# A graph layer on one Trainium2 core: key marks stored tile by tile, keys turned by the tensor engine, and set-up work moved behind the first slot marks

## What is computed

```python
msg = jax.nn.relu(node_inputs[src] + edge_inputs)
agg = jax.ops.segment_sum(msg, dst, num_segments=N_NODES)
h = (1.0 + eps[0]) * node_inputs + agg
x = _layernorm(x + h @ W.T + b, axis=-1)
```

## Time and profile before

| | us |
|---|---|
| median of three runs | 2077.78 (2077.75 to 2079.56) |
| the profiled execution's own time | 2076.23 |
| its span, first to last instruction | 2074.0 |
| PE busy | 2012.9 (97%) |
| PE weight loads | 1920.2 (93%) |
| DVE busy | 1649.0 (80%) |
| ACT busy | 1566.4 (76%) |
| POOL busy | 1517.5 (73%) |

### The profile page before, as it was taken

How to read it: one execution, slowest core, us unless ns; L and a number is a source line. 1 busy time by engine, 2 the same in 40 slices (tenths; PEclk the granted TensorE clock), 3 DMA queues, 4 the chain that set the end, 5 groups by cost and what they waited for, 6 DMA issues and landing times. The chain is left out here.

```text
span 2074.0 us, 117127 instructions
## 1 busy us (share of the span) xinstructions
PE 2012.9 (97%) x46449; PEld 1920.2 (93%) x46449; DVE 1649.0 (80%) x4231; ACT 1566.4 (76%) x1616; POOL 1517.5 (73%) x1571
## 2 busy tenths in 40 slices
PE   2999999999999999999999999999999999999997
PEld 2899999999999999999999999999999999999994
DVE  6888888878888888877888888877888888887885
ACT  5777777777777777777777777777777777777774
POOL 6477777777777777777777777777777777777770
PEclk9999999999999999999999999999999999999998
DMA  6344444444544444444444444444444444444441
GB/s 157 86 112 109 110 111 110 113 114 115 112 111 110 110 111 110 114 112 112 116 111 110 110 110 111 114 113 112 115 112 110 109 110 111 111 115 112 115 112 35
DMA packets 236283, 228.68 MB, mean 110 GB/s; under 512 B 104218, under 2 KB 185556, under 8 KB 236062
## 3 DMA queue, kind: packets, MB, share of 16 engines
q1 hardware_dynamic: 183023, 200.99, 33.5%
q0 software_dynamic: 50080, 25.74, 12.7%
q10 hardware_dynamic: 3154, 1.60, 0.4%
HBM read 225.43 MB, written 2.71 MB: 110 GB/s over the span
## 5 line engine op out<-in xcount | busy, mean ns | idle before, releaser
L536 POOL DMA_INDIRECT rows_all<-in_x,index x1565 | 1517.0, 969 | 507.1 <-issue 474.0
L1173 PE MATMUL found<-table,oh 128*128 128x128 bf16 x18720 | 1241.0, 225 | 11.4 <-issue 3.1
L1173 PEld LDWEIGHTS found<-table,oh 128*128 128x128 bf16 x18720 | 1167.9, 144 | 43.6 <-issue 21.2
L1008 ACT ACTIVATE oh<-keys,minus_lanes 128x1024 bf16<-128x1024 f16 x195 | 224.2, 1150 | 310.3 <-PE found L1173 294.4
L1154 PE MATMUL l<-xparts,oh 128*57 128x96 bf16 x18720 | 436.5, 207 | 0.9 <-ACT oh L996 0.9
L1154 PEld LDWEIGHTS l<-xparts,oh 128*57 128x57 bf16 x18720 | 409.7, 108 | 14.1 <-issue 1.1
L989 ACT ACTIVATE oh<-slots,minus_lanes 128x1824 bf16<-128x1824 f16 x195 | 351.3, 1801 | 0.0
L781 DVE COPY_PREDICATED rows_all<-mask,found 128x256 f32<-128x256 uint16 x780 | 343.3, 440 | 7.6 <-issue 1.4
L964 ACT CAST table<-l 128x768 bf16<-128x768 f32 x390 | 311.1, 798 | 40.2 <-PE l L1154 26.0
L996 ACT ACTIVATE oh<-oh 128x1824 bf16<-128x1824 bf16 x195 | 335.7, 1721 | 0.0
L775 DVE TENSOR_TENSOR mask<-iota,side 128x32 f16<-128x32 f16 x195 | 37.6, 193 | 305.2 <-PE found L1173 290.1
(11 more groups left out here) (126 smaller groups left out, 904.4 us busy)
## 6 DMA issues: line engine op xcount, KB each, us to landing
slots<-slot_dram SPq DMA_DIRECT2D x195, 456.0 KB
msg<-in_edge SPq DMA_DIRECT2D x390, 128.0 KB
keys<-key_dram SPq DMA_DIRECT2D x195, 256.0 KB
rows_all<-in_x,index POOLq DMA_INDIRECT x1565
index<-in_src SPq DMA_DIRECT2D x195, 4.0 KB
key_dram<-key SPq DMA_DIRECT2D x195, 2.0 KB
slot_dram<-slot_row SPq DMA_DIRECT2D x195, 3.6 KB
oh<-in_x SPq DMA_DIRECT2D x3, 512.0 KB, 6.5
```

The costliest lines, as they stand in the source:

```text
L536: pool.indirect_dma_start(to, None, x, bass.IndirectOffsetOnAxis(indices[:, j:j + 1], 0)).then_inc(done, 16)
L1008: nc.scalar.activation(key_marks(b), by_edge(keys[:, four, :]), ACT.Square, bias=minus_lanes[:, b:b + 1]).then_inc(keys_squared, 1)
L1173: last = nc.tensor.matmul(found[:, t * FOUND:(t + 1) * FOUND], key_marks(b)[:, :, t], table[:, b, n * FOUND:(n + 1) * FOUND],  start=(b == ...
```

## The change

Four things are edited together.

- Key marks: `oh2` is now P x KEYS x COLS with no pitch; keys, and so marks, are in order of tile and then edge, so a tile's 128 marks are one run of 256 bytes. DVE and ACT read and write runs.
- Keys on PE: DVE writes the 8 keys into the first 8 of 32 columns of one `key` tile, which has one buffer where it had two. In `fill_slots` PE multiplies it with the identity, which turns it into `key_ps` (32 x 128) beside `slot_ps` in PSUM. ACT copies both at once (32 x 185 where it was 32 x 57). SP writes keys and slots to DRAM after that copy; `spread_keys` is gone. DVE no longer waits for the key write of two rows back; ACT does.
- Set-up order: DVE does `place_nodes` and `prepare_weights` at the end of step -1, behind the slot marks of row 0; the three `describe_chunk` calls move from the ends of steps -2, 0 and 1 to those of 0, 1 and 2. PE's `prepare_weights` moves from step -2 to step 0, behind `look_in_buckets`.
- Loads and clears: the load of x for the output (`x_sb`) moves from ACT's queue to SP's at the end of step -1; ACT's last two `clear_sums` move to the ends of steps 0 and 1.

```diff
-        oh2 = sb("oh2", [P, KEYS, P * PITCH], BF16)
+        oh2 = sb("oh2", [P, KEYS, COLS], BF16)
...
+        key_ps = ranks[0:BUCKETS, 256:256 + P]
+        slot_ps = ranks[0:BUCKETS, 256 + P:256 + P + CAP]
+        turned_ps = ranks[0:BUCKETS, 256:256 + P + CAP]
...
         def key_marks(b):
-            return oh2[:, b, :].rearrange("p (e t) -> p e t", t=PITCH)[:, :, 0:LOOK]
+            return oh2[:, b, :]
...
-            def spread_keys(st):
-                if has(st, 2, ROWS):
...
-                    sp.wait_ge(key_ready, r + 1)
-                    sp.dma_start(key_dram[four].rearrange("(p t) -> p t", t=LOOK), key[:, two, :]).then_inc(key_written, 16)
...
             def spread_slots(st):
...
                     sp.wait_ge(slots_copied, r + 1)
-                    sp.dma_start(slot_dram[four].rearrange("(b c) -> b c", c=CAP), slot_row[:, two, :]).then_inc(slots_written, 16)
+                    sp.dma_start(key_dram[four].rearrange("(t p) -> t p", p=P), turned_row[0:LOOK, two, 0:P]).then_inc(key_written, 16)
+                    sp.dma_start(slot_dram[four].rearrange("(b c) -> b c", c=CAP), turned_row[:, two, P:P + CAP]).then_inc(slots_written, 16)
...
             def step(st):
                 load_index(st)
-                spread_keys(st)
                 load_edges(st)
                 spread_slots(st)
+                if not st.inside and st.s == FROM + 2:
+                    sp.wait_ge(nodes_ready, 2 * SPANS)
+                    for p0, p1 in shares(NP):
+                        sp.dma_start(x_sb[p0:p1, :, :], x_v[p0:p1, :, :]).then_inc(x_loaded, 16)
...
                         split_x()
+                    if st.s == FROM + 2:
+                        place_nodes()
                         prepare_weights()
-                        place_nodes()
-                        describe_chunk(0)
-                    if st.s == FROM + 2:
                         take_all_nodes()
-                    if 0 <= st.s < 2:
-                        describe_chunk(st.s + 1)
+                    if 0 <= st.s < 3:
+                        describe_chunk(st.s)
...
                     act.wait_ge(slots_ready, r + 1)
-                    nc.scalar.copy(slot_row[:, two, :], slot_ps).then_inc(slots_copied, 1)
+                    nc.scalar.copy(turned_row[:, two, :], turned_ps).then_inc(slots_copied, 1)
...
-                    clear_sums(2)
-                    clear_sums(3)
+                if not st.inside and 0 <= st.s < 2:
+                    clear_sums(st.s + 2)
...
-                                found[:, t * FOUND:(t + 1) * FOUND], key_marks(b)[:, :, t],
+                                found[:, t * FOUND:(t + 1) * FOUND], key_marks(b)[:, t * P:(t + 1) * P],
...
                     wait_count(pe, slots_copied, r)
+                    nc.tensor.matmul(key_ps, key[:, :], ident_half[:, :], start=True, stop=True)
                     for t in range(LOOK):
```

More of the change, by code:

```diff
@@ L48, in gnn_kernel @@
     EARLY_KEYS = 2
-    PITCH = LOOK + 2
     WINDOW = 40
@@ L77, in gnn_kernel @@
     ZRING = 4
+    assert LOOK * BUCKETS <= 256 and P + CAP <= 192 and LOOK <= BUCKETS
     assert SHORT <= POOLED and WINDOW <= P and LOOK % 2 == 0
@@ L146, in gnn_kernel @@
         counts = sb("counts", [P, LOOK, BUCKETS], F16)
-        key = sb("key", [P, 2, LOOK], F16)
+        key = sb("key", [P, BUCKETS], F16)
         in_slot = sb("in_slot", [P, LOOK, CAP], F16)
         placed = sb("placed", [P, LOOK, BUCKETS], F16)
-        slot_row = sb("slot_row", [BUCKETS, 2, CAP], F16)
+        turned_row = sb("turned_row", [BUCKETS, 2, P + CAP], F16)
         mask = sb("mask", [P, 2, LOOK, SIDE], F16)
@@ L213, in gnn_kernel @@
         y_sb = xparts[0:NP, :, :, :].rearrange("p b n f -> p (b n f)").bitcast(F32)[:, 0:NT * P].rearrange("p (t c) -> p t c", c=P)
-        src_rows = oh2[:, :, :].rearrange("p b c -> p (b c)").bitcast(I32)[:, 0:2 * COLS].rearrange("p (h c) -> p h c", h=2)
+        src_rows = oh2[:, :, :].rearrange("p b c -> p (b c)").bitcast(I32).rearrange("p (h c) -> p h c", h=2)
         rel_rows = src_f[:, :, :].rearrange("p h c -> p (h c)").bitcast(F16).rearrange("p (h c) -> p h c", h=2)
@@ L228, in gnn_kernel @@
         rank_ps = ranks[:, 0:LOOK * BUCKETS].rearrange("p (t b) -> p t b", b=BUCKETS)
-        slot_ps = ranks[0:BUCKETS, 384:384 + CAP]
+        key_ps = ranks[0:BUCKETS, 256:256 + P]
+        slot_ps = ranks[0:BUCKETS, 256 + P:256 + P + CAP]
+        turned_ps = ranks[0:BUCKETS, 256:256 + P + CAP]
         rank_iota = ranks[:, 448:448 + CAP]
@@ L397, in key_marks @@
         def key_marks(b):
-            return oh2[:, b, :].rearrange("p (e t) -> p e t", t=PITCH)[:, :, 0:LOOK]
-        def by_edge(values):
-            return values.rearrange("p (e t) -> p e t", t=LOOK)
+            return oh2[:, b, :]
         def turned_sources(k):
@@ L476, in load_edges @@
                         sp.dma_start(msg[slot][:, POOLED * D:ROW], one(edge_spans[1], b - 1)).then_inc(edges_loaded[slot], 16)
-            def spread_keys(st):
-                if has(st, 2, ROWS):
-                    r, two, four = st.s + 2, slot_of(st, 2, 2), slot_of(st, 2, RING)
-                    sp.wait_ge(key_ready, r + 1)
-                    sp.dma_start(key_dram[four].rearrange("(p t) -> p t", t=LOOK), key[:, two, :]).then_inc(key_written, 16)
             def spread_slots(st):
@@ L582, in _ @@
             nc.vector.memset(ones[:, :].bitcast(U16), 0x3C00)
+            nc.vector.memset(key[:, :].bitcast(U16), 0)
             nc.vector.memset(one_row[:, :], 1.0)
@@ L737, in give_key @@
                     r = st.s + 2
-                    wait_count(dve, key_written, (r - 1) * 16)
                     dve.wait_ge(rank_ready, r + 1)
-                    nc.vector.tensor_tensor(key[:, slot_of(st, 2, 2), :], of_row(bucket, r), of_row(key_base, r), ALU.add).then_inc(key_ready, 1)
+                    nc.vector.tensor_tensor(key[:, 0:LOOK], of_row(bucket, r), of_row(key_base, r), ALU.add).then_inc(key_ready, 1)
             def give_slots(st):
@@ L765, in mark_keys @@
                     wait_count(dve, blocks_looked, (r - 1) * KEYS + (b + 1))
-                    nc.vector.tensor_scalar(key_marks(b), by_edge(keys[:, four, :]), lanes[:, b:b + 1], None, ALU.is_equal).then_inc(oh2_ready, 1)
+                    nc.vector.tensor_scalar(key_marks(b), keys[:, four, :], lanes[:, b:b + 1], None, ALU.is_equal).then_inc(oh2_ready, 1)
             def mark_sides(st):
@@ L969, in copy_slots @@
                     wait_count(act, slots_written, (r - 1) * 16)
+                    wait_count(act, key_written, (r - 1) * 16)
                     act.wait_ge(slots_ready, r + 1)
-                    nc.scalar.copy(slot_row[:, two, :], slot_ps).then_inc(slots_copied, 1)
+                    nc.scalar.copy(turned_row[:, two, :], turned_ps).then_inc(slots_copied, 1)
             def relu(st):
@@ L1007, in square_keys @@
                     wait_count(act, blocks_looked, (r - 1) * KEYS + (b + 1))
-                    nc.scalar.activation(key_marks(b), by_edge(keys[:, four, :]), ACT.Square, bias=minus_lanes[:, b:b + 1]).then_inc(keys_squared, 1)
+                    nc.scalar.activation(key_marks(b), keys[:, four, :], ACT.Square, bias=minus_lanes[:, b:b + 1]).then_inc(keys_squared, 1)
             def mark_keys(st):
@@ L1032, in step @@
                     round_x(1, x_mid)
-                    act.wait_ge(nodes_ready, 2 * SPANS)
-                    for p0, p1 in shares(NP):
-                        act.dma_start(x_sb[p0:p1, :, :], x_v[p0:p1, :, :]).then_inc(x_loaded, 16)
-                    clear_sums(2)
-                    clear_sums(3)
+                if not st.inside and 0 <= st.s < 2:
+                    clear_sums(st.s + 2)
             steps(act, step)
@@ L1239, in step @@
                 if not st.inside and st.s == 0:
+                    prepare_weights()
                     turn_nodes()
@@ L1253, in step @@
                 if not st.inside and st.s == FROM + 1:
-                    prepare_weights()
                     place_kept()
```

## The result

The changed kernel takes 2130.6 us in the median of four runs (2123.5 to 2135.2) against 2077.8, also of four: a ratio of 1.0248, 95% interval 1.0232 to 1.0264. It is slower; 2046.6 was forecast, with 2077 as the upper end. Its profiled execution has a span of 2121.2 us and a time of 2123.5.

The account below looks back on a forecast made before the run. PE was taken to bound the kernel, with POOL close behind and the bound after the change: 69.2 + 1908.3 + E (30) + 3.3 + 32.0 gave a span of 2042.8 us, 2046.6 as time, range 2027 to 2077.

Parts of the forecast that it names:

- 5.1 forecast: look_in_table on PE: quicker weight loads from runs gain 5.1 ns per matmul (bounds 0 and 7), 0.49 us per step.
- the prediction's reading of it: Weight loads of look_in_table: by the skill's rule stride costs nothing; as a rival, time 2081 us, chance 0.11.
- The start: Set-up before the loop: first look_in_table matmul 10.1 us earlier, 1.6 given back, so POOL's long run gains 8.5 us.
- the 32.4 in that sum: Set-up: the time in us from which PE can look in the buckets, where it was 44.65.
- E: POOL's long run of gathers: time added by hold-ups, 30 us, with 6 below and 81 above as bounds.
- The sum of the prediction: Whole span: 69.2 + 1908.3 + E + 3.3 + 32.0, or 2012.8 + E, giving 2042.8 us.
- 17 for the phase: Part of E once DVE waits for POOL in a fixed phase: 0.1 us in each of 165 steps.
- the 6 of the medians: Lower bound and first part of E: 6 us, as the median gather is 4 ns over the least.
- today's 39 / 192: Hold-ups of gathers in the kernel before, 0.2 us per step, taken as the upper end for the fixed phase.
- that 3.3: From the last gather's end to its use by DVE's addition of gathered rows: an estimated 3.3 us.
- collisions eat it: Rival: L733 or L797 holds up a gather by 0.3 us each step, E = 63, time 2080 us; chance 0.14.
- the loop of the slots: Rival: the slots' way over ACT and SP bounds the step at 10.5 us, time 2134 us; chance 0.10.

Follow-up runs that it names:

- first experiment: The kernel before with only the set-up order of the change (DVE, PE, ACT and SP ahead of the loop): 2072.9 us, ratio 0.9976.
- halves and 6 zeros: The changed kernel with DVE's slot and key marks each cut in two instructions and 6 matmuls of zeros per row on PE: 2098.9 us, ratio 1.0105.

## Why the prediction was wrong

**What held.** The weight loads of L1168 last 98 ns, as L1211's did (ns min/median/max, 400 to 1500 us):

```profile
L1168 PEld LDWEIGHTS found<-table,oh x10062: 95/98/99, 401.4 to 1500.0; 128*128 128x128 bf16 x198
L1168 PE MATMUL found<-table,oh x10061: 218/219/229, 401.4 to 1500.0; 128*128 128x128 bf16 x198
```

The starts of its matmuls are 56.0 ns apart in the mean, 61.2 before, and hardly vary (5% and 95% at 55 and 56, before 57 and 67). That is 5.2 ns for 5.1 forecast, and PE's step 9.714 for 9.73. The Trainium skill (TensorE: Matmul & The Clock Gate, Weight-path perf modes) lists "packed or strided" as the fast load's read pattern and names no difference in time between the two. That they cost the same was the prediction's reading of it, and it does not hold in this case: 142 against 98 ns. The start held as well:

```profile
33.52 0.73 PE L1149 MATMUL l<-xparts,oh 128*57 128x96 bf16 x13 [0.83 <-ACT oh L995]
...
46.67 1.54 PE L1168 MATMUL found<-table,oh 128*128 128x128 bf16 x13 [1.59 <-ACT table L962]
...
69.19 1.19 POOL L534 DMA_INDIRECT rows_all<-in_x,index  x1 [7.36 <-PE found L1168]
```

POOL's long run starts at 69.19 and not 77.74, 8.55 us earlier for 8.5. The way there was less exact: the first L1168 comes at 46.67 and not 45.2 (the 32.4 in that sum should be 28.6 + 3.5 = 32.1; measured is 33.5). That POOL then bounds the kernel and DVE waits for it at L796 also came.

**The term that failed is E**, the hold-ups of the gathers, "E = 6 + 7 + 17 = 30". The sum of the prediction with what was measured: 69.2 + 1908.3 + E + (2121.2 - 2084.7 = 36.5, for 35.3) = 2121.2 gives E = 107: 103 of hold-ups and 4 of a gap behind PE near 94 us, which no part of the sum had:

```profile
94.49 1.16 POOL L534 DMA_INDIRECT rows_all<-in_x,index  x1 [4.39 <-PE found L1168]
```

That is 77 us over the 30, and above the 81 that was called the upper bound. Of the 103, some 15 fall in the first 40 steps, and 88 in the rest, where the sum had 17 for the phase and most of the 6 of the medians. E failed in three ways.

- The list of instructions that hold a gather was too short. I counted L733 and L797, which read two SBUF tiles, and left out the marks by `tensor_scalar` (L753, L765), because in the trace before most gathers that ran beside them were not longer. They were not, because in the phase in which POOL rested against L733 nearly all began too soon after a mark's start: of 154 with 0.16 us or more of a slot mark ahead of them 151 began within 0.016 us of its start, and of 212 at a key mark 189 began 0.067 to 0.079 us after its start. None of these was held. 62 of the 103 us come from marks. The Trainium skill, GPSIMD Engine Reference, Specifications, names both kinds: two SBUF inputs, and instructions in a 2-port perf mode. I took half of that sentence. The trace does not name an instruction's mode; if the marks run in such a one, the 93 hold-ups by L753 and 90 by L765 agree with the rest of it.
- The phase was taken as "today's 39 / 192" at the worst. That 0.2 us is the delay of a POOL that is pushed back to PE's pace and would go faster if let; it is no measure of what DVE does to a POOL that lags. A gather that starts somewhere in an instruction of length L waits L/2, and it does so in L / 1.245 of the cases. Summed over the slot marks (2 x 0.64), the key marks (3 x 0.52), L796 (0.72) and L732 (0.42), the squares over 2 x 1.245 are 0.93 us per step; measured is 103 / 192 = 0.54. POOL's step would be 10.9 by the first and is near 10.5 by the second, not 10.1. So this estimate is 1.7 times too high here: the starts don't fall evenly, and those just behind a mark's start are not held.
- The place of L797 was misjudged, in the rival's own "against". It had DVE wait until 3.3 us behind the last gather, between two starts; that 3.3 was borrowed from the landing of the slot load. In the changed kernel the addition begins 1.51 us behind the end of the batch's last gather (median of 134 steps from row 60 on). The second gather after that one begins after 0.305 + 0.94 + 0.305 = 1.55 us, so the addition falls right on a gather's start: in the step above at 1012.77 against 1012.79. When it comes some 0.05 us or more ahead, it holds the gather: 73 times, 0.44 us each in the mean.

The rival "collisions eat it" was the right mechanism with too small a price. Its 0.3 us per step were 0.54, and the time from there 2012.8 + 103 + 4 + 3.5 = 2123, that of the profiled run (the 3.5 are 1.2 of a longer end and 2.3 from the span to the time). The rival whose time fits best, the loop of the slots with 2134, is wrong: with seven gathers the same loop runs at 9.714. ACT waits for slots once in the changed kernel (7.1 us, at the start) and three times with seven gathers (9.2 us in all, 7.3 of it in one wait). A number that fits is no proof of its cause.

Small errors: "never slower that I can see" was said of the key marks; L765 takes 541 ns in the mean for 495 before, since POOL and DVE hold each other up. The start's gain reached POOL in full, but with the loop unchanged only 4 of 8.5 us are left at the end (first experiment).

## What to carry to other kernels

An engine whose gaps are all "issue" and all alike (0.305 us between gathers here) has no slack in them: add the gap to each instruction before you call the next engine the bound, and ask at what pace the present bound hides it. Where two engines share a path, a lagging one can cost more than a slower first one; here six matmuls of zeros, 0.33 us more of PE per step, make the changed kernel 3.4% faster (0.9903 / 1.0248). Before a bound is handed to an engine that shares a path, sum over the instructions that can hold it, each with its length squared over twice the pace (1.7 times too high here, but nearer than a phase guessed from before), and take none out because it did no harm in the old phase.

## What was not expected of the hardware

- Each hold-up ends with one DVE instruction: the gather's end lies 0.815 us (within 0.025 in 268 of 268) behind that instruction's end. In other runs most do, not all: 197 of 198 in the kernel before, some 350 of 400 with halves and 6 zeros. It must have begun a little before the gather, and how much differs: L796 holds from 0.047 us on and not up to 0.044, the key mark L765 from 0.073 on and not up to 0.076. The addition at 1012.77, 0.02 us ahead of the gather at 1012.79 (0.95 us), does not hold it.
- The 98 gathers that began in the first 0.076 us of a key mark and were not held made the mark longer: 0.53 us where it is 0.48 beside a gather that it holds. A mark that begins some 0.5 us into a gather lasts 0.66.
- The step is stable where POOL would be faster than PE (by twenties of rows, from row 20 to row 180: 10.158 to 10.162 with 8 zeros, 10.046 to 10.050 with 6), and wanders from 9.83 to 10.63 where it is slower.
- Two chips run the same program 46 and 48% slower, with PE waiting for "issue" inside its trains. Why is open.
